# Products of the division and of the context moved from VectorE to GpSimd, in a one-core RWKV decoder layer with newly laid lists of steps

## What is computed

```python
x = x + attn(layernorm(x))      # k, v, r = projections of a mix of each token and the one before it
                                # out = (e1*aa + e2*v) / (e1*bb + e2), a scan over the tokens
                                # Wo @ (sigmoid(r) * layernorm(out))
x = x + wkv(w, u, layernorm(x), ctx)    # the same kind of scan, k = layernorm(x), v = ctx
h = silu(x @ gate.T * gs) * (x @ up.T * us)
x = x + (h @ down.T) * ds
```

## Time and profile before

| | |
|---|---|
| median of three runs | 600.77 us (599.24 to 601.04) |
| profiled execution | 598.28 us |
| its span, first to last instruction | 596.4 us |
| PE busy | 536.3 us, 90% |
| DVE busy | 457.1 us, 77% |
| ACT busy | 345.4 us, 58% |
| POOL busy | 53.4 us, 9% |
| mean granted clock of TensorE | 0.960 |

### The profile page before, as it was taken

How to read it: one execution, slowest core, us unless ns; L and a number is a source line. 1 busy time by engine, 2 the same in 40 slices (tenths; PEclk the granted TensorE clock), 3 DMA queues, 4 the chain that set the end, 5 groups by cost and what they waited for, 6 DMA issues and landing times.

```text
span 596.4 us, 8018 instructions
## 1 busy us (share of the span) xinstructions
PE 536.3 (90%) x2658; PEld 381.6 (64%) x2658; DVE 457.1 (77%) x742; ACT 345.4 (58%) x546; POOL 53.4 (9%) x155
## 2 busy tenths in 40 slices
PE   2998589677799999999889999999969999999995
PEld 2443444323398446885689446786768699989994
DVE  5999778996977489999857589999856499852433
ACT  4737783467868257676557447766644486634221
POOL 2000300101022003000103003000011100000000
PEclk9999699988989999999979999999979999999998
DMA  8999700012100000001060000001040010010001
GB/s 304 414 315 385 291 0 2 18 35 87 48 26 2 1 1 0 1 19 53 1 213 0 0 0 1 0 18 53 0 142 0 1 38 36 0 36 1 2 36 38
DMA packets 14261, 39.02 MB, mean 65 GB/s; under 512 B 1232, under 2 KB 1232, under 8 KB 14032
## 3 DMA queue, kind: packets, MB, share of 16 engines
q1 hardware_dynamic: 14224, 38.57, 18.0%
HBM read 34.37 MB, written 12.85 MB: 79 GB/s over the span
## 4 chain that ended last, share of the span: by engine, by line
issue 38%; PE 34%; DVE 15%; POOL 6%; ACT 5%; DMA 1%; DVEq 0%; POOLq 0%; SPq 0%; ACTq 0%
PE gu L722 13%; PE dacc L650 7%; PE bank L636 6%; PE bank L698 5%; PE bank L625 3%; POOL t_rstd L598 2%; DVE t_slot L954 2%; DVE t_st L1091 1%; ACT L745 1%; DVE t_slot L1099 1%; DVE t_otile L1149 1%; DVE t_slot L1046 1%; POOL t_veps L596 1%; ACT t_z L799 1%; DVE t_xf L1116 1%
## 5 line engine op out<-in xcount | busy, mean ns | idle before, releaser
L722 PE MATMUL gu<-t_z4h,t_gate 128*128 128x256 f32 x352 | 94.1, 299 | 7.9 <-DVE t_z4l L1123 7.5
L722 PE MATMUL gu<-t_z4l,t_gate 128*128 128x256 f32 x352 | 89.3, 286 | 0.0
L722 PE MATMUL gu<-t_z4l,t_up 128*128 128x256 f32 x352 | 89.3, 286 | 0.0
L722 PE MATMUL gu<-t_z4h,t_up 128*128 128x256 f32 x352 | 89.2, 285 | 0.0
L879 ACT ACTIVATE t_h<-gu,t_fsc 128x256 f32<-128x256 f32 x88 | 40.4, 472 | 67.3 <-PE gu L722 65.8
L722 PEld LDWEIGHTS gu<-t_z4h,t_gate 128*128 128x128 f32 x352 | 68.4, 194 | 12.7 <-issue 10.4
L650 PE MATMUL dacc<-t_down,t_hh 128*128 128x512 f32 x176 | 72.5, 412 | 1.8 <-DVE t_hl L973 1.8
L722 PEld LDWEIGHTS gu<-t_z4l,t_gate 128*128 128x128 f32 x352 | 68.3, 194 | 2.4 <-issue 1.7
L650 PE MATMUL dacc<-t_down,t_hl 128*128 128x512 f32 x176 | 69.0, 392 | 0.0
L1128 DVE SCALAR_TENSOR_TENSOR t_h<-gu,t_fsc,t_h 128x256 f32<-128x256 f32 x88 | 40.6, 476 | 36.0 <-ACT t_h L879 35.9
L722 PEld LDWEIGHTS gu<-t_z4h,t_up 128*128 128x128 f32 x352 | 68.1, 193 | 0.0
(11 more groups left out here) (129 smaller groups left out, 930.5 us busy)
## 6 DMA issues: line engine op xcount, KB each, us to landing
t_mixv<-in_x SPq DMA_DIRECT2D x8, 512.0 KB, 6.0
t_xres<-in_x SPq DMA_DIRECT2D x8, 512.0 KB, 5.5
t_ctxt<-in_ctx_t SPq DMA_DIRECT2D x16, 256.0 KB, 2.8
out<-t_otile SPq DMA_DIRECT2D x16, 256.0 KB, 2.2
gate_words<-in_gate_t SPq DMA_DIRECT2D x1, 2816.0 KB, 17.1
up_words<-in_up_t SPq DMA_DIRECT2D x1, 2816.0 KB, 24.3
t_gate<-gate_words SPq DMA_DIRECT2D x1, 2816.0 KB, 15.5
down_words<-in_down_t SPq DMA_DIRECT2D x1, 2816.0 KB, 23.1
```

The costliest lines, as they stand in the source:

```text
L722: last = pe.matmul(gu[u % 2][:, side, :], as_read(w[:, k, i * P:(i + 1) * P], exact), as_read(part[:, k, hf * HALF:(hf + 1) * HALF], exact ...
```

## The change

Three kinds of edit:

- The first instruction of `refine` (L954, the products of numerator and denominator with the reciprocal) and `xin` (L1079, the exponential times the context) are now issued by POOL, with the same operands and sizes. DVE keeps the second instruction of `refine` (L956), which waits for POOL's semaphore.
- All lists but POOL_LAST, SP_NEXT and SP_LAST are laid out anew. In PE_FIRST `return2` stands behind `v0+` and `y` behind `v3+`. In SP_FIRST the load of the down weights (`words2`) stands ahead of the second half of the next x (`xload1+`).
- `rw` waits in addition for `tanh_done`, and `fin` for `mix_done`.

```diff
     POOL_FIRST = """
-        rn0 rn1 rn2 rn3 rn0+ rn1+ nb4 rn4 nb5 rn5 nb6 rn6
+        rn0 rn1 fin0 fin1 fin2 fin3 rn2 rn3 rn0+ rn1+ fin0+ nb4 rn4 nb5 rn5 fin1+ xin0 xin1 xfin0 xfin1
+        xin2 xin3 xfin2 xfin3 nb6 rn6 fin2+ fin3+
     POOL_BODY = """
-        nb7 rn7 rn2 rn3 rn0 rn1 nb4 rn4 nb5 rn5 nb6 rn6
+        nb7 rn7 rn2 rn3 rn0 rn1 fin0 fin1 fin2 fin3 nb4 nb5 rn4 rn5 xin0 xin1 xfin0 xfin1 xin2 xin3
+        xfin2 xfin3 nb6 rn6
     PE_FIRST = """
-        turn1 k0 k1 v0 v1 k2 k3 v2 v3 r0 r1 r2 r3 turn2 return2 turn1+ k0+ k1+ v0+ wo v1+ turn3 r0+ r1+
-        r2+ r3+ y k2+ k3+ v2+ v3+ turn4_0 flag
+        turn1 k0 k1 v0 v1 k2 k3 v2 v3 r0 r1 r2 r3 turn2 turn1+ k0+ k1+ v0+ return2 v1+ wo r0+ turn3 r1+
+        flag r2+ r3+ k2+ k3+ v2+ v3+ y turn4_0
     SP_FIRST = """
-        words1 xload0+ xload1+ words2 ctx2 ctx3
+        words1 xload0+ words2 xload1+ ctx2 ctx3
...
+            def quotient(b, c, reciprocal, square):
+
+                need(pool, reciprocal, b, c + 1)
+                pool.tensor_tensor(slot[:, c % 2, 2:4, :], slot[:, c % 2, 1::2, :],
+                                   slot[:, c % 2, 0:1, :].to_broadcast([P, 2, T]), ALU.mult).then_inc(square, 1)
...
+                if s.startswith("fin"):
+                    quotient(b, k, rec_done, refine_done)
+                elif s.startswith("xfin"):
+                    quotient(b, k, xrec_done, xrefine_done)
+                elif s.startswith("xin"):
+                    need(pool, ctx_in[k % 2], b, 16 * (k // 2 + 1))
+                    need(pool, xexp_done, b, k + 1)
+                    pool.tensor_tensor(slot[:, k % 2, 2, :], slot[:, k % 2, 0, :], ctxt[:, k % 2, :], ALU.mult).then_inc(inp_done, 1)
...
-            def refine(b, c, dst, reciprocal, square, result):
+            def refine(b, c, dst, square, result):
 
                 sl = slot[:, c % 2]
-                both = slot[:, c % 2, 1::2, :]
-                need(dve, reciprocal, b, c + 1)
-                dve.tensor_tensor(slot[:, c % 2, 2:4, :], both, slot[:, c % 2, 0:1, :].to_broadcast([P, 2, T]), ALU.mult).then_inc(square, 1)
                 need(dve, square, b, c + 1)
```

More of the change, by code:

```diff
@@ L100, in decoder_layer @@
+        xpart0 xpart1 xfront2 tanh1+ tanh2+ xfront3 xpart2 xpart3 tanh3+ front2+ front3+ sq6 part2+
+        norm6 part3+ z4_0_0 z4_0_1 flag
         """.split()
     ACT_BODY = """
[L103 to L106, removed]
@@ L122, in decoder_layer @@
+        z4_1_1 silu9 high4 silu10 silu11 high5 silu12 silu13 high6 silu14 silu15 silu16 silu17 high7
+        silu18 silu19 high8 silu20 high9 silu21 high10
         """.split()
     DVE_FIRST = """
-        stat1_0 stat1_1 norm0 norm1 mixk0 mixk1 mixk2 mixk3 mixv0 mixv1 mixv2 mixv3 mixr0 front0 front1
-        nv0 mixr1 mixr2 nv1 den0 num0 part0 den1 num1 mixr3 part1 fin0 front2 fin1 front3 nv2 den2 num2
-        nv3 part2 den3 num3 part3 fin2 fin3 stat2_0 stat2_1 norm2 norm3 stat1_0+ stat1_1+ norm0+ rw0 rw1
@@ L128, in decoder_layer @@
[L128 to L132, removed]
@@ L133, in decoder_layer @@
-        fin2+ fin3+
+        stat1_0 stat1_1 norm0 norm1 mixk0 mixk1 mixk2 mixk3 mixv0 mixv1 mixv2 mixv3 front0 front1 den0
+        nv0 num0 mixr0 nv1 part0 mixr1 den1 num1 part1 mixr2 fin0 mixr3 front2 fin1 front3 nv2 den2 num2
+        part2 nv3 den3 num3 part3 fin2 fin3 stat2_0 stat2_1 stat1_0+ stat1_1+ norm2 norm3 norm0+ norm1+
+        mixk0+ mixk1+ mixk2+ mixk3+ mixv0+ mixv1+ mixv2+ mixv3+ front0+ front1+ nv0+ rw0 rw1 den0+ rw2
+        mixr0+ rw3 num0+ part0+ den1+ nv1+ num1+ part1+ weigh x1_0 x1_1 x1_2 mixr1+ mixr2+ mixr3+ x1_3
@@ L134, in decoder_layer @@
+        norm4 norm5 fin0+ xfront0 fin1+ xfront1 xden0 xnum0 xpart0 xden1 xnum1 xpart1 xfin0 xfront2
+        xden2 xfin1 xfront3 xnum2 xpart2 xden3 xnum3 xpart3 xfin2 front2+ xfin3 front3+ den2+ nv2+ nv3+
+        num2+ xf_0 xf_1 part2+ den3+ num3+ part3+ norm6 flag xf_2 xf_3 z4_0_0 z4_0_1 fin2+ fin3+
         """.split()
     DVE_BODY = """
-        norm7 prod0 z4_1_0 z4_1_1 prod1 prod2 rest0 stat2_0 stat2_1 prod3 norm2 norm3 stat1_0 prod4
-        prod5 stat1_1 rw0 rw1 norm0 rw2 norm1 mixk0 mixk1 rest1 mixk2 rw3 mixk3 mixv0 mixv1 mixv2 mixv3
@@ L139, in decoder_layer @@
-        x1_0 x1_1 x1_2 x1_3 front0 rest2 front1 den0 nv0 num0 prod6 prod7 part0 den1 mixr0 mixr1 fin0
-        mixr2 nv1 mixr3 num1 norm4 part1 front2 fin1 prod8 prod9 front3 rest3 nv2 den2 num2 prod10
-        prod11 part2 rest4 den3 nv3 prod12 num3 rest5 prod13 norm5 part3 out0 fin2 out1 xfront0 prod14
-        prod15 fin3 xfront1 rest6 xin0 xden0 xnum0 prod16 xpart0 xin1 xden1 xnum1 prod17 xpart1 xfin0
-        xfront2 xfin1 xfront3 rest7 rest8 xin2 xden2 xnum2 prod18 xpart2 xin3 xden3 xnum3 prod19 xpart3
@@ L144, in decoder_layer @@
-        rest9 xfin2 xfin3 prod20 prod21 xf_0 xf_1 rest10 out2 norm6 xf_2 out3 z4_0_0 xf_3 z4_0_1
+        norm7 prod0 z4_1_0 z4_1_1 prod1 rest0 stat2_0 stat2_1 prod2 stat1_0 prod3 norm2 norm3 prod4
+        prod5 stat1_1 norm0 rest1 norm1 prod6 prod7 mixk0 mixk1 mixk2 mixk3 mixv0 mixv1 mixv2 front0 rw0
+        mixv3 rest2 den0 front1 nv0 num0 nv1 part0 den1 num1 part1 rw1 rw2 mixr0 mixr1 fin0 fin1 front2
+        front3 nv2 rw3 prod8 nv3 den2 num2 part2 den3 num3 part3 x1_0 mixr2 fin2 mixr3 rest3 prod9 x1_1
```

95 lines of the change are left out of this document (47 added, 48 removed).

## The result

The changed kernel takes 636.42 us in the median against 600.74 us: ratio 1.0613, 95% interval 1.0594 to 1.0633. It is slower by 6%, or 36 us. The profiled execution spans 634.5 us against 596.4.

What follows compares the result with a forecast made beforehand. PE was taken to bound the rounds and last stretch, DVE often the first stretch. Terms +2.3, +5.4 and +0.5 gave +8.2 us on 598.28: 606.5 us profiled, 609.0 us median with 2.5 us added; range 590 to 630 us.

Steps and rivals of the forecast that it cites:

- the lock: On the SBUF ports DVE and POOL share: held for a whole instruction, the loser blocks fully.
- blocked share: Share of POOL's product time that DVE loses: 0.55, a little under the 62% of its stream that can be blocked.
- the waits for products: After a batch's last `part3` or `xpart3`, `fin3` and `xfin3` come 1.3 us later; +2.6 us in the first stretch, +1.3 per round.
- the lists' gain: First stretch: new PE order covers up to 5.7 us of gaps, less 3.3 us given back, so -2.4 us.
- Price of a product: On POOL: 2.3 ns a column, so 2.5 us for 1024 columns and 1.3 us for 512.
- little shelter: Behind `part0` in DVE's list stand steps with two SBUF operands, then `fin0`, which waits for the product anyway; no separate size.
- The give-back for `xload1+`: First stretch: loading the second half of x behind `words2` delays `stat1_1+` and the norms behind it; 3.3 us given back.
- "`y` behind `v3+` gains nothing in the end": First stretch: `norm6` stands behind `part3+`, so DVE's batch 1 work comes first; no gain.
- The rounds: Two rounds: DVE +1.4 us and delay at `y` +1.3 us, so +2.7 us each, +5.4 us together.
- The last stretch: DVE +0.8 us plus a delayed finish, mostly covered by PE's stock of work as `y` has no wait: +0.5 us.
- The rival with share 0.9: The lock holds nearly whole: about 643 us if all reaches the end, taken as 628 us; chance 0.13.
- The rival in which the products run beside DVE: POOL's products run beside DVE or are shorter: faster, 593 us, or 587 us at share 0; chance 0.30.

Runs made afterwards that it cites:

- the first run: The changed kernel's new lists, with all products issued by DVE as before: 619.37 us, ratio 1.0317 against the kernel before.
- the extra products: Kernel before, with 48 extra GpSimd products that nobody reads at the change's places, nothing taken off DVE: 649.63 us, ratio 1.0817.
- four columns: GpSimd's products cut to four columns, the rest left out: changed kernel 594.13 us; kernel before with the offload in its old lists 592.29 us.

## Why the prediction was wrong, point by point

The direction was right: 57% on slower, with the lock as the reason. The size was not: 609.0 us with a range to 630, where 636.4 was measured. The sum had +10.6 us for the offload and -2.4 for the lists. Taken in the order of the first run, lists and then offload, the runs have +19 and +17: the lists are 21 of the 27 us that the forecast fell short. In the other order they have +40 for the offload and -4 for the lists, and all of the miss is the offload's. So no single term carries the miss. The step that failed is the adding up: lists and offload were each priced against the gaps of the old kernel, as if the other were not there. Within it failed the blocked share, the waits for products and the lists' gain, as follows.

- **Price of a product.** Taken at 2.5 and 1.3 us; bare it is 2.34 (the fastest of 32) and 1.28. Right. With DVE's instructions in its way the mean was 2.64 and 1.71.
- **Blocked share.** This term was mis-sized. I took 0.55, a little under the 62% of DVE's stream that can be blocked. The bare products are 32 x 2.34 + 16 x 1.28 = 95.4 us, so the changed kernel's share is 70.6 / 95.4 = 0.74. Without the new lists it is 44.7 / 95.4 = 0.47, and with products that nobody needs 0.55. So the share as I took it fits the old lists; what I left out is that the new ones place dense two-operand work under the products. I had even written down that `mixr1 den1 num1 part1 mixr2` stand there, and drew "little shelter" from it but no higher share. With 0.74 for 0.55 my own sum gives +27.5 us, 628 us; 8 us are still missing, most of it in the first and the last stretch.
- **The waits for products.** I priced them as tails, 1.3 us each, once at the end of a batch. That was the second failure: with the offload in the old lists DVE waits 40.8 us in all, at 15 places. Of the 15 waits 12 are 2.2 to 3.2 us long, about a whole product: `fin` and `xfin` stand where the reciprocal is just ready, in the middle of a batch as well as at its end. In the changed kernel 7.8 us of it are left; the rest became share. Share and wait have to be priced together: 0.8 to 0.9 us of loss for each microsecond of product in both lists.
- **The lists.** The prediction gave them -2.4 us in the first stretch and nothing in the rounds; alone they cost 19 us, 10.1 of them in the first stretch. The step that failed is the look for gaps on PE that the new order could fill, without a look at whether DVE's new order delivers in time. `turn1+` alone got a gap of 10.48 us, where it and `return2` had 5.7 together. The give-back for `xload1+` was right in kind and size: 3.3 us predicted, 3 measured by the run that undoes it, and PE's order won nothing to set against it. But `k0+` started at 80.9 us, not near 76.5.
- **"`y` behind `v3+` gains nothing in the end".** Right for the lists with the products on DVE (618.12 us put back, of which the load is 3 us, against 619.37). Wrong for the changed kernel, where putting it back costs 6.5 us, in part because it bares a wait for a product where I had priced one tail.
- **The rounds.** Predicted +2.7 us each with `y` waiting 3 us; measured +7.5 and +8.4 with `y` waiting 0.33. The delay is taken earlier in the round. The waits of PE in that stretch, of which only the first two stood there before:

```profile
PE bank L690 <- DVE t_z L961: 2.1, 1, 2.1
PE gu L737 <- DVE t_z4l L1130: 1.7, 1, 1.7
PE bank L713 <- DVE t_slot L1030: 1.5, 1, 1.5
PE gu L737 <- DVE t_h L1135: 1.4, 2, 0.9
PE bank L651 <- DVE t_mixk L975: 1.2, 1, 1.2
PE bank L640 <- ACT t_tanh_r L843: 1.2, 1, 1.2
```

  Of the 7.5 us the new lists cost 3.7 alone. PE reaches `y` as late as DVE does. Looking for a delay only at the place that waited before was wrong.
- **The last stretch.** Predicted +0.5, measured +8.8. PE's stock of work did not cover it: 15.2 us of products fall here too, and I let "`y` has no wait" stand for the whole stretch. The lists alone make it 4.7 us longer, the offload alone 10.9.
- **The rival with share 0.9** gave 643 us if all reached the end, and I took 628 on the ground that a part falls into waits that are there anyway. In the old lists that ground fails: there a net loss comes out nearly whole. In the new ones it holds, 17.0 of 28.6 us. That 628 is nearer to 636.4 than my point is luck in part, since 0.9 is more than was measured and the lists' own cost is not in it. The range should have gone to 643.
- **The rival in which the products run beside DVE** is excluded by the extra products. Its ceiling was about right: 587 to 593 us forecast, 594.1 measured with four columns in the new lists and 592.3 in the old.

## What to carry to other kernels

Before work is moved from VectorE to GpSimd, ask of every VectorE instruction that would run beside it whether it reads two operands from SBUF, or copies or scales from SBUF to SBUF. Here each microsecond of product cost DVE 0.8 to 0.9 us, against a relief of 0.52 us (49.8 / 95.4), so the exchange lost in both orders tried. Filling the wait with other VectorE work helped where that work had an operand in PSUM. Copies and `tensor_scalar` with their one operand in SBUF were caught, and the batch statistics, the last kind, never stood beside a product. A plan that counts the engines as independent lays blocked work under the products.

Price new lists together with the load that they are made for: the same lists cost 19 us without the offload and gained 4 us with it.

If GpSimd must read beside a dense VectorE, short instructions were better than long ones (8 to 9 us here). And where a net loss of an engine reaches the end whole but a net gain only in part, as in the old lists, the range of a forecast should be wider on the slow side.

## What the runs showed of the hardware

- A GpSimd memset of 1404 columns in bf16 took 1.26 us each time, with no effect on VectorE's two-operand instructions beside it, nor they on it. But it shut out five two-column copies from SBUF to SBUF for its whole length, 1.30 us each.
- GpSimd's undisturbed product took 0.72, 1.28 and 2.34 us for 256, 512 and 1024 columns: some 0.2 us, and 2.1 ns a column.
- A copy of two columns on VectorE took up to 2.25 us (mean 0.73, before 0.14) when it was caught by a product. Its shortness did not save it.
- With slices of 0.72 us on one side and instructions of 0.7 to 1.2 us on the other, a slice took 1.09 us in the mean and VectorE's instructions ended 0.3 to 0.5 us late in the stretch shown; that would fit turns of one instruction each, though no view here shows each turn.
